# V projection of a cross-attention kernel as five fp32r products, with nine maxima jobs moved in among the x transposes and Q products

## The reference

```python
x = x + xattn(layernorm(x), ctx)     # x 2048 x 256, ctx 1601 x 192, 16 heads of 64
x = x + ffn(layernorm(x))

# xattn: x = layer_norm(x) * g_norm; q = x @ Wq; k, v = split(ctx @ Wkv)   Wkv is 192 x 2048
#   one learned null key and null value stand before the 1601 keys of each head
#   out = softmax(q k^T / 8, masked) @ v @ Wout, then a layer norm with g_out
# ffn: three layers with weights of +1 and -1, relu between them
```

## Time and profile before

| | us |
|---|---|
| median of 3 runs | 1311.0 (1309.39 to 1314.98) |
| the profiled execution | 1310.91 |
| its span, first to last instruction | 1309.1 |
| the head on PE, first K product to the end of the last V part | 15.27 to 94.12 |
| PE busy in the span | 1279.7 (98%) |

### The profile page before, as it was taken

The page is one execution under the profiler, slowest core; times in us unless marked ns, Lnnn a source line. Parts: engine busy times, 40 slices in busy tenths (PEclk is TensorE's granted clock), DMA queues, the critical chain, the costliest instruction groups (busy, mean ns, idle before and its releaser), DMA issues.

```text
span 1309.1 us, 20514 instructions
## 1 busy us (share of the span) xinstructions
PE 1279.7 (98%) x7316; PEld 685.7 (52%) x7316; DVE 828.9 (63%) x1214; ACT 914.1 (70%) x1176; POOL 944.2 (72%) x480
## 2 busy tenths in 40 slices
PE   6999999999999999999999999999999989999998
PEld 3334444444444444444444444444444648787876
DVE  5456767666767666676667676666775675453532
ACT  3338889888878888898888788888888553414242
POOL 0008899999999999999999999999999731010100
PEclk9999999999999999999999999999999999999999
DMA  6242011200210121112102110211432110210000
GB/s 165 65 129 76 26 34 41 68 33 34 82 34 34 35 74 33 34 40 68 34 34 70 45 36 33 75 34 34 126 106 98 49 57 10 97 65 17 1 17 17
DMA packets 59735, 70.59 MB, mean 54 GB/s; under 512 B 14321, under 2 KB 42036, under 8 KB 59636
## 3 DMA queue, kind: packets, MB, share of 16 engines
q1 hardware_dynamic: 53780, 64.17, 15.2%
q10 hardware_dynamic: 5856, 5.11, 1.2%
HBM read 51.57 MB, written 17.69 MB: 53 GB/s over the span
## 4 chain that ended last, share of the span: by engine, by line
PE 93%; DVE 2%; ACT 2%; issue 1%; DMA 0%; SPq 0%; DVEq 0%; ACTq 0%
PE ps_ox L1548 28%; PE ps_s L1535 23%; PE ps_ox L1403 10%; PE ps_ox L1651 8%; PE ps_s L1651 4%; PE ps_ox L1463 4%; PE ps_s L1623 3%; PE ps_s L1388 2%; PE ps_ox L1452 2%; PE ps_ox L1454 2%; PE ps_s L1390 2%; PE ps_ox L1485 1%; PE ps_ox L1408 1%; PE ps_ox L1420 1%; ACT hf L1013 1%
## 5 line engine op out<-in xcount | busy, mean ns | idle before, releaser
L954 ACT ACTIVATE prob<-ps_s,keybias 128x1024 f32<-128x1024 f32 x416 | 440.9, 1110 | 115.7 <-PE ps_s L1535 115.3
L1548 PE MATMUL ps_ox<-prob,vp 128*64 128x512 f32 x1664 | 403.4, 605 | 0.0
L736 POOL TENSOR_TENSOR acc<-acc,prob 128x1024 f32<-128x1024 f32 x163 | 389.9, 2392 | 10.6 <-ACT prob L954 8.9
L1128 DVE TENSOR_REDUCE mxh<-ps_ox 128x2 f32<-128x1024 f32 x244 | 299.2, 1226 | 148.4 <-PE ps_ox L1403 145.2
L934 ACT ACTIVATE ps_s<-shift 128x512 f32<-128x512 f32 (+1 forms) x400 | 309.3, 814 | 0.0
L736 POOL TENSOR_TENSOR acc_odd<-acc_odd,prob 128x1024 f32<-128x1024 f32 x120 | 286.0, 2383 | 5.4 <-ACT prob L954 5.4
L1548 PEld LDWEIGHTS ps_ox<-prob,vp 128*64 128x64 f32 x1664 | 101.0, 136 | 189.6 <-issue 142.1
L1535 PE MATMUL ps_s<-qh,kh 64*128 64x512 f32 x832 | 174.5, 414 | 4.8 <-DVE ps_s L1233 2.9
L1403 PE MATMUL ps_ox<-kh,qh 64*128 64x512 f32 x746 | 170.9, 451 | 0.8 <-ACT vsb L848 0.7
L1233 DVE COPY ps_s<-shift 128x512 f32<-128x512 f32 (+1 forms) x216 | 155.8, 724 | 19.3 <-ACT prob L954 19.1
L1535 PE MATMUL ps_s<-ql,kh 64*128 64x512 f32 x832 | 166.7, 393 | 0.0
(11 more groups left out here) (166 smaller groups left out, 1417.0 us busy)
## 6 DMA issues: line engine op xcount, KB each, us to landing
shift<-m_scratch SPq DMA_DIRECT2D x32, 512.0 KB, 3.7
rb<-r_scratch SPq DMA_DIRECT2D x64, 128.0 KB, 2.9
o_scratch<-o_sb SPq DMA_DIRECT2D x32, 256.0 KB, 2.0
otb<-o_scratch SPq DMA_DIRECT2D x4, 2048.0 KB, 8.0
v_scratch<-vsb SPq DMA_DIRECT2D x13, 512.0 KB, 3.2
vp<-v_scratch SPq DMA_DIRECT2D x8, 832.0 KB, 5.1
xs<-in_x SPq DMA_DIRECT2D x4, 512.0 KB, 6.7
xres<-in_x ACTq DMA_DIRECT2D x1, 2048.0 KB, 8.1
```

What stands on the lines that cost most here:

```text
L736: gp.tensor_tensor(sum_to, terms[0], terms[1], ALU.add).then_inc(sums_p, 1)
L954: act.activation(prob[:, slot(u, s), :, :], ps_s[s % S_BUFS][:, :, :], ACT.Exp, bias=keybias[:, kt:kt + 1], scale=SCALE).then_inc(p_made, 1)
L1128: dve.reduce_max(mxh[:, :, i // MXF, i % MXF], ps[:, :, 0:MXW], AX.X).then_inc(x_free, 1)
L1548: last = pe.matmul(ps_o[qb % 2][rows(g), :], vp[u][:, kt, rows(g)], prob[:, slot(u, s), g, :], start=(kt == 0), stop=(kt == KT - 1))
```

## The change

- V is no longer projected in fp32. Each operand is split into an fp32r high part and an fp32r low part, and V is the sum of five fp32r products: part 0 is now three (`chi0` by `whi[0]`, `clo0` by `whi[0]`, `chi0` by `wlo[0]`), part 1 two over 128 rows that hold the 64 remaining inputs twice, high parts above low parts (`c1` by `whi[1]`, `c1` by `wlo[1]`).
- A new job `P` makes the parts: ACT copies the high part (`high_part`), DVE subtracts to get the low part (`low_part`). Six of them: `T1 0` and `T3 0` (768 columns of `cT0` and `cT1`), `W 0`, `W 1` (1024 columns), `T1 1`, `T3 1` (896 columns), one or two ahead of each K job. The first V part waits for the first four low parts, half tile 12 for all six.
- `wv1` is loaded twice, into the upper and the lower 64 partitions. The null value is not projected any more: two DMAs write it straight into its row of `v_dram`, and the last V tile is stored by two DMAs around that row. The load of `vp[0]` waits for these too.
- The order of the head: no V part between the K jobs, 12 after K 3; two or three behind each x transpose and Q product, and in the second to fourth group of these a maxima job between the two (nine in all). The 14 other maxima jobs follow with the last 13 V parts, one behind each but the last.
- The first ten maxima jobs all use `ps_x`, and each waits for the `reduce_max` of the one before it; from the eleventh on two buffers alternate.
- On DVE `normalise(1)` and the rest of the layer norm come behind K 3. On ACT the two last roots come behind the copies of V half tiles 2 and 4.

```diff
@@ -59,7 +60,10 @@
 
 CT_N = (KT + 1) // 2
 XT_N = QT // 2
-V_BESIDE_K = [0, 2, 2, 3]
+V_FIRST = 12
+HEAD_BESIDE_Q = 9
+V_CUT = 6 * P
+PARTS = {0: [("T1", 0), ("T3", 0)], 1: [("W", 0)], 2: [("W", 1)], 3: [("T1", 1), ("T3", 1)]}
@@ -129,23 +133,28 @@
     values = iter([("V", h, part) for h in range(2 * KT) for part in range(2)])
     order = [("CT", i) for i in range(CT_N)]
     for c in range(4):
-        order += [("K", c)] + [next(values) for _ in range(V_BESIDE_K[c])]
+        order += [("P",) + part for part in PARTS[c]] + [("K", c)]
+    order += [next(values) for _ in range(V_FIRST)]
+
+    ahead = iter([("SA",) + job for job in maxima_jobs(0, 0, True)] + [("SA",) + job for job in maxima_jobs(0, 1)[:HEAD_SA]])
 
     def queries(c):
-        return [("XT", 2 * c), next(values), ("XT", 2 * c + 1), next(values), ("Q", c), next(values)]
+
+        out = []
+        for job in (("XT", 2 * c), ("XT", 2 * c + 1), ("Q", c)):
+            out += [job, next(values), next(ahead) if c else next(values), next(values)]
+        return out
 
     for c in range(4):
         order += queries(c)
-    for job in maxima_jobs(0, 0, True):
-        order += [("SA",) + job, next(values)]
-    for job in maxima_jobs(0, 1)[:HEAD_SA]:
-        order += [("SA",) + job, next(values)]
-        if job[3] == 0:
+    for job in ahead:
+        order += [job] + list(islice(values, 1))
+        if job[1:] == maxima_jobs(0, 1)[0]:
             order += [("MX", 0)]
...
         def head_x(j):
 
-            return ps_s[0] if j % 2 else ps_x
+            return ps_s[0] if j >= HEAD_BESIDE_Q and j % 2 == 0 else ps_x
...
@@ -539,10 +556,9 @@
                              null_kv[0:1, :].unsqueeze(1).broadcast_to([1, 2, HD])).then_inc(ld_null_k, 16)
             load_pair_weights(sp, 0, 0)
             load_x(1)
-            sp.dma_start(wv1[row + 1:row + 2, :].rearrange("a (h d) -> a h d", h=HEADS),
-                         null_kv[1:2, :].unsqueeze(1).broadcast_to([1, HEADS, HD])).then_inc(ld_null_v, 16)
             sp.dma_start(wv0[:, :], wkv[0:P, INNER:2 * INNER]).then_inc(ld_wv, 16)
-            sp.dma_start(wv1[0:CDIM - P, :], wkv[P:CDIM, INNER:2 * INNER]).then_inc(ld_wv, 16)
+            for r in range(2):
+                sp.dma_start(wv1[rows(r), :], wkv[P:CDIM, INNER:2 * INNER]).then_inc(ld_wv, 16)
             load_x(2)
             load_x(3)
...
             def store_v(kt):
                 sp.wait_ge(vh_free, 2 * (kt + 1))
-                sp.dma_start(v_dram[:, :, kt, :].rearrange("r p d -> p r d"),
-                             vsb[kt % 2][:, :].rearrange("p (r d) -> p r d", d=P)).then_inc(v_stored[kt % 2], 16)
+                keys = slice(0, NULL_ROW if kt == NULL_TILE else P)
+                sp.dma_start(v_dram[:, keys, kt, :].rearrange("r p d -> p r d"),
+                             vsb[kt % 2][keys, :].rearrange("p (r d) -> p r d", d=P)).then_inc(v_stored[kt % 2], 16)
+                if kt == NULL_TILE:
+                    sp.dma_start(v_dram[:, NULL_ROW + 1:P, kt, :].rearrange("r p d -> p r d"),
+                                 vsb[kt % 2][NULL_ROW + 1:P, :].rearrange("p (r d) -> p r d", d=P)).then_inc(v_rest, 16)
...
+            for g in range(2):
+                sp.dma_start(v_dram[:, NULL_ROW, NULL_TILE, rows(g)],
+                             null_kv[1:2, :].broadcast_to([PAIRS, HD])).then_inc(v_null, 16)
...
             for r in range(2):
                 sp.wait_ge(v_stored[r], 16 * ((KT + 1 - r) // 2))
+            sp.wait_ge(v_rest, 16)
+            sp.wait_ge(v_null, 32)
             sp.dma_start(vp[0][:, :, :], v_dram[0]).then_inc(v_loaded[0], 16)
...
+            def high_part(what, r):
+
+                cols = slice(V_CUT, KPAD) if r else slice(0, V_CUT)
+                if what == "W":
+                    act.wait_ge(ld_wv, 48)
+                    act.activation(whi[r][:, :], (wv1 if r else wv0)[:, :], ACT.Copy).then_inc(v_hi, 1)
+                elif what == "T1":
+                    act.wait_ge(tr_free, CT_N)
+                    act.activation(chi0[:, cols], cT0[:, cols], ACT.Copy).then_inc(v_hi, 1)
+                else:
+                    act.activation(c1[rows(0), cols], cT1[rows(0), cols], ACT.Copy).then_inc(v_hi, 1)
+
...
                 elif job[0] == "V":
                     if job[2]:
                         evac_v(job[1])
+                        if job[1] in (2, 4):
+                            root()
                 elif job[0] != "SA":
                     spare(0, n, ("MX", 0, 0) if job[0] == "MX" else (job[0], 0, job[1]), None)
-                    if job in (("K", 1), ("K", 2)):
-                        root()
                     if job == ("K", 3):
...
+            low_parts = iter(range(1, 7))
+
+            def low_part(what, r):
+
+                dve.wait_ge(v_hi, next(low_parts))
+                cols = slice(V_CUT, KPAD) if r else slice(0, V_CUT)
+                if what == "W":
+                    dve.tensor_tensor(wlo[r][:, :], (wv1 if r else wv0)[:, :], whi[r][:, :].bitcast(F32), ALU.subtract).then_inc(v_lo, 1)
+                elif what == "T1":
+                    dve.tensor_tensor(clo0[:, cols], cT0[:, cols], chi0[:, cols].bitcast(F32), ALU.subtract).then_inc(v_lo, 1)
+                else:
+                    dve.tensor_tensor(c1[rows(1), cols], cT1[rows(0), cols], c1[rows(0), cols].bitcast(F32), ALU.subtract).then_inc(v_lo, 1)
+
             statistics(0)
             statistics(1)
             normalise(0)
-            normalise(1)
-            beside_k = {0: lambda: statistics(2), 1: lambda: statistics(3), 2: lambda: normalise(2), 3: lambda: normalise(3)}
             for j, job in HEAD:
                 if job[0] == "K":
                     rest_of_keys(job[1], j, None)
-                    beside_k[job[1]]()
+                    if job[1] == 3:
+                        statistics(2)
+                        statistics(3)
+                        for c in range(1, 4):
+                            normalise(c)
+                elif job[0] == "P":
+                    low_part(*job[1:])
                 elif job[0] == "Q":
                     rest_of_queries(job[1], j, None)
...
                 keys, cols = slice(kt * P, (kt + 1) * P), slice(half * 512, (half + 1) * 512)
                 if part == 0:
                     if h == 0:
-                        pe.wait_ge(ld_wv, 32)
-                        pe.wait_ge(ld_null_v, 16)
+                        pe.wait_ge(v_lo, 4)
+                    if h == 2 * (V_CUT // P):
+                        pe.wait_ge(v_lo, 6)
                     if h >= 2:
                         pe.wait_ge(vh_free, h - 1)
-                    pe.matmul(ps_v[h % 2], cT0[:, keys], wv0[:, cols], start=True, stop=False)
+                    pe.matmul(ps_v[h % 2], chi0[:, keys], whi[0][:, cols], start=True, stop=False)
+                    pe.matmul(ps_v[h % 2], clo0[:, keys], whi[0][:, cols], start=False, stop=False)
+                    pe.matmul(ps_v[h % 2], chi0[:, keys], wlo[0][:, cols], start=False, stop=False)
                 else:
-                    pe.matmul(ps_v[h % 2], cT1[:, keys], wv1[:, cols], start=False, stop=True).then_inc(vh_made, 1)
+                    pe.matmul(ps_v[h % 2], c1[:, keys], whi[1][:, cols], start=False, stop=False)
+                    pe.matmul(ps_v[h % 2], c1[:, keys], wlo[1][:, cols], start=False, stop=True).then_inc(vh_made, 1)
...
+                elif job[0] == "P":
+                    continue
                 elif job[0] == "SA":
-                    if n == 1:
+                    if n == HEAD_BESIDE_Q + 1:
                         pe.wait_ge(tr_free, CT_N + XT_N)
-                    if n >= 2:
-                        pe.wait_ge(x_free, n - 1)
+                    if n >= 1:
+                        pe.wait_ge(x_free, n if n <= HEAD_BESIDE_Q else n - 1)
                     maxima(n, job[1:], None, head_x(n))
```

More of the change, by code:

```diff
@@ L9 @@
 from contextlib import ExitStack
+from itertools import islice
 import concourse.bass as bass
@@ L147, in plan_head @@
     for job in order:
-        if job[0] in ("CT", "XT", "V"):
+        if job[0] in ("CT", "XT", "V", "P"):
             out.append((None, job))
@@ L321, in xattn_ffn_kernel @@
         wv0 = sb("wv0", [P, INNER], region="head")
-        wv1 = sb("wv1", [C1, INNER], region="head")
+        wv1 = sb("wv1", [P, INNER], region="head")
         vsb = [sb(f"vsb{r}", [P, INNER], region="head") for r in range(2)]
@@ L361, in xattn_ffn_kernel @@
         fT = [sb(f"fT{m}", [P, QW], region="shift") for m in range(DC)]
+        at["parts"] = end_all
+        chi0, clo0, c1 = [sb(name, [P, KPAD], F32R, region="parts") for name in ("chi0", "clo0", "c1")]
+        assert at["parts"] <= at["odd"]
+        at["parts"] = at["odd"] + FF * 4
+        whi = [sb(f"whi{r}", [P, INNER], F32R, region="parts") for r in range(2)]
+        wlo = [sb(f"wlo{r}", [P, INNER], F32R, region="parts") for r in range(2)]
+        assert at["parts"] <= at["late"]
```

(7 more changed lines are left out.)

## The result

| | before | changed |
|---|---|---|
| median, us | 1310.22 (1309.31 to 1314.98, 6 runs) | 1303.86 (1302.49 to 1305.58, 6 runs) |
| profiled span, us | 1309.1 | 1300.6 |
| K 0 starts | 15.27 | 15.80 |
| last V part ends | 94.12 | 81.98 |
| load of `vp[0]` issued | 98.15 | 92.13 |

The ratio is 0.9941, 95% interval 0.9927 to 0.9954: faster by 0.6%. The forecast was 1295.5 with a range of 1291.5 to 1300.5. Its sign was right, its size was not, and the time lies outside the range. V ended 12.1 us earlier, but the loop's second product with V is only 4.8 us earlier. The rest was lost in the hand-over between the two. The end of the last V part is read as 0.23 us behind the start of its last pass (0.86 with fp32).

The account below looks back on a forecast made before the run. PE's queue in the head was taken as the bound: 15.3 + 0.4 + 0.4 + 0.6 - 1.0 - 0.7 = 15.0 us to V's end, then the hand-over, gain 15.4; 1310.9 - 15.4 = 1295.5 us, range 1291.5 to 1300.5.

Parts of the forecast that it names:

- The V products: Head: a half tile takes five fp32r passes, 1.13 us, instead of 1.72; 26 half tiles save 15.3 us.
- The rival of a slow fp32r pass: V products in the head: a pass takes 0.43 us like fp32, time 1323; chance 0.04.
- Switches of shape: Head: four fewer switches between K and V save 0.4 us; gaps around the maxima jobs stay.
- The K stretch: Head, K jobs: making the parts on DVE delays K 2 and K 3; PE loses 1.0 us, V starts near 22.1.
- that rival: K stretch costs more, as the clock falls or DVE comes later: 3.4 us lost, time 1297 to 1300.5; chance 0.18.
- Roots, "PE has two banks ahead of it": Head, ACT: roots behind V copies 2 and 4 hold its queue up to 1 us; PE has two banks ahead.
- The rival that all stores are slow: V stores in the head: at 8.5 us each, V ends 9 us later, time 1305; chance 0.04 with other waits.
- The tenth maxima job: Head: it follows the ninth after one V part with a single buffer, so PE waits 0.7 us.
- The last V part at 79.1: End of V in the head: 15.0 us earlier than before, at 79.1 us.
- The hand-over: Head to loop: a second store adds 0.4 us, load of `vp[0]` lands at 88.5, product with V starts at 88.6.
- The forecast's own sign of being wrong: Hand-over: a product with V that starts over 10 us after the last V part.
- PE's own way: Hand-over: last maxima job, reduce, seed, then 7.0 us as before; first product with V at 88.6 at most.

## Why the prediction was wrong

- **What bounds the kernel: right.** A gain on PE in the head moved what followed, as far as no other wait took its place; PE is as full in the loop as before (51.99 of 52 us busy again from 140 to 192).
- **The V products, 15.3 us: right.** Passes of 0.23 us. The rival of a slow fp32r pass is out.
- **Switches of shape: about right.** The gaps beside maxima jobs are as before (V, maxima, V at 40.65, 40.97, 41.39 with 0.34 for the first pass); a half tile of five passes takes 1.13 to 1.16 us.
- **The waits before Q: right.** All four are gone.
- **The K stretch, 1.0 us lost: nearly.** K 2 waited 0.81 (0.75 said) and K 3 0.25 (0.2). V began at 23.05, not 22.1: 0.5 of this is K 0's later start, 0.4 is DVE's queue. The later start is not the change's as far as the runs show: the kernel before, profiled again, had K 0 at 16.03. The granted clock was 1.00 from 16 to 24 us, so that rival is out.
- **Roots, "PE has two banks ahead of it": wrong**, by 1.15 us. ACT was held for 1.23 us as said, but each V half tile is only 1.13 us of PE work now, and the copy behind the root came too late for the bank after next.
- **Stores of 3.2 us a tile: right** up to tile 11. The rival that all stores are slow is out.
- **The tenth maxima job, 0.7 us: right** (0.80). The last stretch ran at 1.21 us for a pair, 1.2 said.
- **The last V part at 79.1: 2.9 us late** (81.98): 0.5 K 0, 0.4 DVE, 1.15 ACT, 0.1 the tenth job. The remaining 0.7 would fit 130 passes of 0.232 instead of 0.2266 us; no run isolates it.
- **The hand-over, "a second store is issued ahead of it, 0.4 us more": this is the step that failed.** It was priced by SP's issue time alone, on top of the 4.03 us that the kernel before needed with stores of 128 rows, as if a store of 62 rows would land like these. Its own duration, on two DMA engines, put the load 10.15 us behind the last V part where 4.43 were said. PE waited 4.77 us (0 said), and the granted clock was 0.50 for 6.8 us from within that wait on. Taken away, this brings 7.1 us, and the time into the range: 1296.75, with 1295.5 forecast. No rival had it: the one about stores took all of them to be equally slow, and the range had nothing for a DMA of an odd shape. The forecast's own sign of being wrong did come, a product with V over 10 us behind the last V part: it was 14.7 us. But that sign was set too near, since without the slow store it still was 9.7 to 11.5.
- **How the miss adds up.** The forecast means a second product at 92.6 (88.6 and the 4.04 us between the two before) and a span of 1293.7. It came at 103.26, 10.6 us late: 2.9 from V's end, 5.2 on the way to the first product, which is the wait of 4.77 and little more, and 2.6 behind it at the low clock. From there on this execution was 3.7 us shorter than the one that the forecast was built on, so the span missed by 6.9; the median lies another 1.4 us above this execution.
- **That 1296.75 lies so near to 1295.5 is in part luck.** There V ended 3.2 us and the second product came 4.1 us later than forecast, and the stretch behind took 1197.7 us where the forecast, without saying so, had carried over the 1201.0 of its one profile.
- **PE's own way, 9.5 us from the last V part to the first product: undersized** in four of the five executions without the slow store (9.7 once, 10.5 to 11.5 in the others). The forecast let the low clock in as it had been before, and it can hold for longer.

A trace of before could not show the price, since it has no store of 62 rows. The warning was in the diff: a DMA whose number of rows changed from 128 to 65 and 62, on the one chain that leads from the last V part to the loop.

## What to carry to other kernels

When a change cuts a DMA, price each piece by its own number of rows and not by the bytes or by the whole DMA before: with 62 rows in one store the load behind went out 9.3 us after the first store was issued, with 48 and 14 rows after 4.3. Look first at the DMA that ends last on the way to the next stage, and give it a row count that 16 divides, as 48 and 128 here, or move the odd rest to where nobody waits. In a queue that runs strictly in order, a small instruction that waits for another engine costs everything behind it; put it behind the work that PE needs.

## What the runs showed of the hardware

- A store of 248 KB in 512-byte runs: 62 rows at a time moved at 44 GB/s (DMA share 0.15), 31 rows at a time at 22 GB/s (0.07). Two such stores of 31 rows one behind the other took the same engine: the DMA share stayed at 0.07 with both issued, and the load behind them waited until 98.16, as an estimate of 496 packets of 27 ns on one engine had given (27 ns from the 340 packets that took 14.3% of 16 engines' time between 87 and 91 us of the changed kernel).
- PE idle for 4.77 us came out of it at a granted clock of 0.50, which held until about 102.3 us: the first product with V took 3.6 us instead of 1.9, and the second came 6.6 us after it (4.04 before). The Trainium skill, "TensorE: Matmul & The Clock Gate", Part 1, has activity as what lifts the clock; the trace agrees in that the clock rose again while PE was busy. The wait alone does not explain the low clock: in the four executions with the 62 rows stored ahead and the maxima jobs moved the second product came 4.7 to 5.15 us after the first with no wait for the load, and 4.03 in the one with the maxima jobs in their old place, which stayed at 1.00. What decides it is not shown.
- In single executions of the same kernel the low clock comes or stays away late in the loop (near 1015 and 1050 us), so two profiled spans can differ by some 3 us with no difference between the kernels. From the second product with V to the end it was between 1197.0 and 1201.0 us in all twelve profiled executions. Spans of two profiles should be compared by stage.
